# Second message pass of a two-layer GNN and FFN kernel: rows copied by VectorE into fixed buffers, ring slots freed by the last item that uses them

## The reference

```python
# src, dst: 50000 edges, sorted by dst; N = 3125 nodes, 256 features
def _L1_gnn_ref(x, W, b, edge_index):
    src, tgt = edge_index
    xt = jnp.einsum('ni,oi->no', x, W) + b
    out = jax.ops.segment_sum(xt[src], tgt, num_segments=N)
    deg = jax.ops.segment_sum(jnp.ones_like(tgt), tgt, num_segments=N)
    return out / (deg + 1.0)[:, None]

x = x + _L1_gnn_ref(_layernorm(x), W, b, [src, dst])
```

## Time and profile before

| | |
|---|---|
| timed runs (3) | median 2085.95 us, 2084.43 to 2091.15 |
| profiled execution, first to last instruction (span) | 2418.4 us |
| PE / DVE / ACT / POOL busy in the span | 57% / 39% / 19% / 46% |
| second message pass, first gather to last add | 1563.44 to 2189.47 us, 626.0 us |

### The profile page before, as it was taken

How to read it: one execution, slowest core, us unless ns; L and a number is a source line. 1 busy time by engine, 2 the same in 40 slices (tenths; PEclk the granted TensorE clock), 3 DMA queues, 4 the chain that set the end, 5 groups by cost and what they waited for, 6 DMA issues and landing times. The chain is left out here.

```text
span 2418.4 us, 23547 instructions
## 1 busy us (share of the span) xinstructions
PE 1368.5 (57%) x6436; PEld 1105.6 (46%) x6436; DVE 932.4 (39%) x1860; ACT 449.9 (19%) x1265; POOL 1109.8 (46%) x1085
## 2 busy tenths in 40 slices
PE   2512555555546136649999567035463434367988
PEld 1311433444434125549999566013342323245767
DVE  7512433333333387513333123713222222236853
ACT  0111333333334013213333122000000000002320
POOL 4276666666651400463322722173666665631530
PEclk7755667767668565679999778557666767678988
DMA  5463867677665701341111111731333332310002
GB/s 122 118 180 107 270 212 246 229 252 240 223 225 181 195 7 50 111 123 37 62 49 37 61 37 42 178 105 57 94 90 93 90 94 77 94 50 1 0 1 53
DMA packets 155861, 271.60 MB, mean 112 GB/s; under 512 B 23387, under 2 KB 118161, under 8 KB 154625
## 3 DMA queue, kind: packets, MB, share of 16 engines
q0 software_dynamic: 46128, 123.83, 17.2%
q1 hardware_dynamic: 91516, 127.72, 16.6%
q10 hardware_dynamic: 18103, 18.59, 3.4%
HBM read 172.86 MB, written 98.14 MB: 112 GB/s over the span
## 5 line engine op out<-in xcount | busy, mean ns | idle before, releaser
L1119 PE MATMUL bank<-sum_rows,sum_hot 128*125 x896 | 279.6, 469 | 384.5 <-issue 300.9
L1098 POOL DMA_INDIRECT sum_rows<-xn_tab,src_e x392 | 372.6, 951 | 271.0 <-issue 111.3
L739 POOL DMA_INDIRECT gat_rows<-xh_tab,src_e x364 | 349.1, 959 | 196.4 <-issue 103.6
L1119 PEld LDWEIGHTS bank<-sum_rows,sum_hot 128*125 128x125 f32 x896 | 193.9, 231 | 468.0 <-issue 437.4
L811 PE MATMUL bank<-gat_rows,gat_same 128*128 128x264 f32 x784 | 280.5, 500 | 171.8 <-issue 166.6
L811 PEld LDWEIGHTS bank<-gat_rows,gat_same 128*128 128x128 f32 x784 | 179.6, 250 | 218.4 <-issue 178.5
L1145 DVE TENSOR_TENSOR sums<-sums,bank 125x256 f32 x224 | 94.3, 421 | 452.5 <-remote 258.9
L1719 PE MATMUL bank<-weights,e_xthigh 128*128 x896 | 225.1, 334 | 59.2 <-issue 53.8
L855 ACT COPY gat_outs<-bank 128x264 f32<-128x264 f32 x392 | 145.8, 382 | 311.4 <-PE bank L811 231.2
L1719 PEld LDWEIGHTS bank<-weights,e_xthigh 128*128 128x128 f32 x896 | 157.6, 196 | 70.5 <-issue 70.5
L1841 DVE TENSOR_TENSOR e_h<-e_gated,bank 128x342 f32<-128x342 f32 x112 | 57.1, 510 | 335.1 <-ACT e_gated L1789 309.7
(11 more groups left out here) (483 smaller groups left out, 2320.9 us busy)
## 6 DMA issues: line engine op xcount, KB each, us to landing
parts<-gat_outs SPq DMA_DIRECT2D x28, 1904.0 KB
staged<-w_tab SPq DMA_DIRECT2D x8, 2132.0 KB
w_tab<-w_stage SPq DMA_DIRECT2D x16, 682.0 KB
w_raw<-in_L_ffn_w_dram SPq DMA_DIRECT2D x16, 640.0 KB
gat_rows<-xh_tab,src_e POOLq DMA_INDIRECT x392
sum_rows<-xn_tab,src_e POOLq DMA_INDIRECT x392
w_tab<-w_stage SPq DMA_DIRECT2D x8, 768.0 KB
w_raw<-in_L_ffn_w_dram SPq DMA_DIRECT2D x8, 682.0 KB
```

The costliest lines, as they stand in the source:

```text
L739: pool.indirect_dma_start(out=rows[b % R][:, t, :], out_offset=None, in_=k.xh_tab, in_offset=bass.IndirectOffsetOnAxis(ap=k.src_e[:, b * S ...
L1098: pool.indirect_dma_start(out=rows[:, at // IP % (RING * GPAIRS), at % IP, :], out_offset=None, in_=k.xn_tab, in_offset=bass.IndirectOffse ...
L1119: m = nc.tensor.matmul(k.ps[s][0:P, 0:C], hot[u][:, s, c, :], rows[:, bass.ds(slot, 1), c, :].rearrange("p a c -> p (a c)"), start=(c == 0 ...
```

## The change

DVE copies the two row blocks of each item (128 x 512 elements, fp32) from its ring slot into one of seven fixed buffers `held`; PE reads `held` and `hot` at constant addresses and has no register loads left. DVE does this in `stage(n)`, seven items ahead of the adds: first seven copies, then one behind each add. The reading of slot and batch and the wait for `landed` move from PE to DVE, in front of the copy; the batch is now read for every fourth item. The ring slot is free when the last item that uses the batch is staged: `walk_room` holds that item's number + 1 for each batch, and SP, three batches later (`AHEAD`), reads it, waits for `staged`, and raises `room`, on which POOL waits. The eight copies of `Prep` that ACT made go to DVE. `walk_room` costs one DVE instruction over 49 elements in the phase before.

```diff
+        v.tensor_scalar(self.room[:, :], self.ends[0:1, GPAIRS - 1:PAIRS:GPAIRS], 1.0, None, ALU.add)
...
-    def on_scalar(self, act):
-        s_, att = self.k.nc.scalar, self.k.att
-        for j in (0, 1, 2, 3, 4, 5, 12, 13):
-            act.wait_ge(self.made, j + 1)
...
+        if j < 2:
+            v.tensor_copy(self.wt[:, j, :], self.room[:, :]).then_inc(self.kept, 1)
+        elif j < 6:
+            v.tensor_copy(self.w_xt[:, j - 2, :], self.room[:, :]).then_inc(self.kept, 1)
+        elif j >= 12:
+            v.tensor_copy(att["bias"][:, (j - 12) * C:(j - 11) * C], self.room[0:P, :]).then_inc(self.kept, 1)
...
+        held = sb("held", [EP, IB, IP, C])
...
+        def wait_landed(eng, n):
+            last = min(n + LAND, ISLOTS) - 1
+            eng.wait_ge(landed, eng.value_load(w.batch[0:1, last:last + 1], min_val=1, max_val=GBATCHES))
...
             for b in range(GBATCHES):
+                if b >= AHEAD and b - AHEAD < GBATCHES - RING:
+                    sp.wait_ge(staged, sp.value_load(w.room[0:1, b - AHEAD:b - AHEAD + 1], min_val=1, max_val=ITEMS))
+                    sp.sem_inc(room, 1)
                 sp.wait_ge(rows_in[b % RING], 16 * GB * (b // RING + 1))
                 sp.sem_inc(landed, 1)
...
                 if b >= RING:
-                    pool.wait_ge(sums, GPAIRS * (b - RING) + GPAIRS - 1 + NT)
+                    pool.wait_ge(room, b - RING + 1)
...
-                        slot = pe.value_load(w.slot[0:1, n:n + 1], min_val=0, max_val=RING * GPAIRS - 1)
-                        if s % LAND == 0:
-                            last = n + min(LAND, IB - s) - 1
-                            pe.wait_ge(landed, pe.value_load(w.batch[0:1, last:last + 1], min_val=1, max_val=GBATCHES))
-                        pe.wait_ge(added, n + 1)
-                        for c in range(IP):
-                            m = nc.tensor.matmul(k.ps[s][0:P, 0:C], hot[u][:, s, c, :], rows[:, bass.ds(slot, 1), c, :].rearrange("p a c -> p (a c)"),
-                                                 start=(c == 0), stop=(c == IP - 1))
...
+                    pe.wait_ge(added, n + 1)
+                    pe.wait_ge(staged, n + 1)
+                    for c in range(IP):
+                        m = nc.tensor.matmul(k.ps[s][0:P, 0:C], hot[g % 2][:, s, c, :], held[:, s, c, :], start=(c == 0), stop=(c == IP - 1))
+                    m.then_inc(sums, 1)
...
+            def stage(n):
+                pair = ring_pair(dve, n)
+                if n % LAND == 0:
+                    wait_landed(dve, n)
+                dve.wait_ge(sums, n + 1)
+                v.tensor_copy(held_pair(n), pair).then_inc(staged, 1)
...
+                    dve.wait_ge(sums, n + 1 + IB)
                     dve.wait_ge(added, n + IB)
                     into = tile_of(k.sums, node)
                     v.tensor_tensor(into, into, k.ps[s][0:P, 0:C], ALU.add).then_inc(added, 1)
+                    if n + IB < ISLOTS:
+                        stage(n + IB)
```

More of the change, by code:

```diff
@@ L873 @@
 LAND = 4
+AHEAD = 3
 HD = 64
@@ L889, in __init__ @@
         self.slot, self.node, self.batch = sb("slot", [1, ISLOTS], I32), sb("node", [1, ISLOTS], I32), sb("batch", [1, ISLOTS], I32)
+        self.room = sb("room", [1, GBATCHES], I32)
         self.consts, self.lasts, self.reached, self.summed, self.found, self.spread, self.picked, self.laid = (
@@ L1046, in on_vector @@
         j = self.step_before(g)
-        if j is None or not 6 <= j < 12:
+        if j is None:
             return
@@ L1075, in sum_phase @@
         rows = sb("rows", [EP, RING * GPAIRS, IP, C])
+        held = sb("held", [EP, IB, IP, C])
         hot = [sb(f"hot{s}", [EP, IB, IP, P]) for s in range(2)]
         rows_in = [k.gather_sem(f"sum_rows_in{s}") for s in range(RING)]
-        landed, hot_made, sums, added, lanes = (sem(n) for n in ("landed", "hot_made", "sums", "added", "lanes"))
+        landed, staged, room, hot_made, sums, added, lanes = (
+            sem(n) for n in ("landed", "staged", "room", "hot_made", "sums", "added", "lanes"))
         lane = k.ps[IB][:, 0:P]
@@ L1082, in sum_phase, with ring_pair, held_pair @@
         block = ctx.enter_context(nc.Block())
+        def wait_landed(eng, n):
+            last = min(n + LAND, ISLOTS) - 1
+            eng.wait_ge(landed, eng.value_load(w.batch[0:1, last:last + 1], min_val=1, max_val=GBATCHES))
+        def ring_pair(eng, n):
+            slot = eng.value_load(w.slot[0:1, n:n + 1], min_val=0, max_val=RING * GPAIRS - 1)
+            return rows[:, bass.ds(slot, 1), :, :].rearrange("p a i c -> p (a i c)")
+        def held_pair(n):
+            return held[:, n % IB, :, :].rearrange("p i c -> p (i c)")
         @block.sync
@@ L1102, in _ @@
         def _(pe):
[L1103 to L1112, removed]
-                        slot = pe.value_load(w.slot[0:1, n:n + 1], min_val=0, max_val=RING * GPAIRS - 1)
-                        if s % LAND == 0:
-                            last = n + min(LAND, IB - s) - 1
-                            pe.wait_ge(landed, pe.value_load(w.batch[0:1, last:last + 1], min_val=1, max_val=GBATCHES))
-                        pe.wait_ge(added, n + 1)
-                        for c in range(IP):
-                            m = nc.tensor.matmul(k.ps[s][0:P, 0:C], hot[u][:, s, c, :], rows[:, bass.ds(slot, 1), c, :].rearrange("p a c -> p (a c)"),
-                                                 start=(c == 0), stop=(c == IP - 1))
-                        m.then_inc(sums, 1)
-        @block.scalar
-        def _(act):
-            prep.on_scalar(act)
+            pe.sem_inc(sums, IB)
+            for g in range(ITURNS):
+                pe.wait_ge(hot_made, g + 1)
+                j = prep.step_before(g)
+                if j is not None:
+                    pe.wait_ge(added, g * IB + 1)
+                    prep.on_tensor(pe, j)
+                for s in range(IB):
+                    n = g * IB + s
+                    pe.wait_ge(added, n + 1)
[3 more added lines that the diff above has]
+                    m.then_inc(sums, 1)
         @block.vector
@@ L1130, in _, with mark, add @@
             dve.sem_inc(added, IB)
[L1132 to L1134 removed]
+            def mark(g):
+                v.tensor_tensor(hot[g % 2][:, :, :, :], lane.rearrange("p (a b n) -> p a b n", a=1, b=1).to_broadcast([EP, IB, IP, P]),
+                                w.local[:, g * IB:(g + 1) * IB, :].rearrange("p i (c n) -> p i c n", n=1).to_broadcast([EP, IB, IP, P]),
                                 ALU.is_equal).then_inc(hot_made, 1)
[L1137 removed]
+            def stage(n):
[4 more added lines that the diff above has]
+                v.tensor_copy(held_pair(n), pair).then_inc(staged, 1)
+            def add(g):
                 prep.on_vector(dve, g)
@@ L1145, in add @@
                     v.tensor_tensor(into, into, k.ps[s][0:P, 0:C], ALU.add).then_inc(added, 1)
+                    if n + IB < ISLOTS:
+                        stage(n + IB)
             v.tensor_copy(lane, k.lane[:, 0:P]).then_inc(lanes, 1)
             dve.wait_ge(lanes, 1)
-            mark(0, 0)
-            for i in range(ITURNS // 2 - 1):
-                mark(i * 2 + 1, 1)
-                add(i * 2, 0)
-                mark(i * 2 + 2, 0)
-                add(i * 2 + 1, 1)
-            mark(ITURNS - 1, 1)
-            add(ITURNS - 2, 0)
-            add(ITURNS - 1, 1)
+            mark(0)
+            for n in range(IB):
+                stage(n)
+            for g in range(ITURNS):
+                if g + 1 < ITURNS:
+                    mark(g + 1)
+                add(g)
 def gather_rows(pool, into, table, row, rows_in, tiles):
```

15 lines of the change are left out of this document (2 added, 13 removed).

## The result

| | median (range), us | runs |
|---|---|---|
| before | 2084.43 (2081.66 to 2091.15) | 5 |
| changed | 2096.75 (2091.64 to 2103.73) | 5 |

The ratio is 1.0076, with a 95% interval of 1.0056 to 1.0096: slower by 0.76%. That is 12 us by the medians and 16 us by the ratio; +24 was forecast, and 2098 to 2135 us for the case that the forecast took for its own.

A forecast was written before the change was run, and what follows sets the result against it. POOL's gathers bound the phase: gathers 490 + 8, landing 2 and drain 23 make 523 us against 504, plus 5 for two engines waiting on each other. That is +24 us, 2085.95 + 24 = 2110 us; range 2000 to 2170.

The forecast's parts named there:

- the case that the forecast took for its own: Whole kernel: spells only in profiles, gathers bound, change slower at 2098 to 2135 us; chance 0.37.
- the ring of two engines: POOL and DVE waiting for each other in the ring lose 5 us where their stalls don't coincide.
- PE's register work is hidden behind the gathers: In timed runs PE needs 1.10 us per item, gathers deliver one in 2.23, so removing register work gains nothing.
- The port: DVE's copies beside POOL's gathers: 8 us more for POOL; rival at full price +107 us, 2193 us, chance 0.07.
- The drain: Behind the last landing: 8 copies, two batch reads, 15 adds and a `mark` on DVE, 23 us against 12.
- the landing: From the end of the eighth gather to PE's start, at the start of the phase: 2 us.
- The steps of `Prep`: 14 steps passing through DVE, 1.6 us each with PE's item behind, 22 us of DVE time.
- PE's spells: Stretches where PE takes 7.0 us per item instead of 1.10; taken for a cost of profiling, absent from timed runs.
- The prediction's test for itself: Signs: profiled phase 626 to 525 to 535 us, POOL's waits 99 to under 30, yet no gain in timed runs.
- Nothing to be seen: Rival: a quarter of the spells real, or chain hidden and port free; within 6 us of 2086; chance 0.14.
- the spells are in the timed runs: Rival: PE's slow stretches are real, phase 626 to 530 us, -96 us, 1990 us; chance 0.29.
- VectorE as the bound: Rival: gathers closer than 1.25 us in timed runs, DVE's 474 us decide; +40 to +98 us; chance 0.13.

The follow-up runs named there:

- idle_copies: Kernel before plus one unneeded 128 x 512 SBUF copy on DVE behind each add: 2432.78 us, ratio 1.0040 to before.
- fixed_all: Changed kernel with tile, slot, batch and room taken from the item's number, so DVE and SP load no register: 2085.66 us, ratio 1.0001 to before.
- fixed_tile: Changed kernel with each item's tile fixed at build time, one load chain less on DVE: 2097.01 us, ratio 1.0050 to before.
- copy_act_c: Changed kernel with row copies, their loads and landing waits moved from DVE to ACT, in the condition 2085: 2081.81 us, ratio 0.9992 to before.
- before_again: Kernel before, unchanged, profiled a second time, in the condition 2420: 2401.72 us (1 run), beside 2420.64 for before.
- before_c: Kernel before, unchanged, profiled a third time, in the condition 2085: 2083.17 us (1 run), beside 2084.00 for before.
- half_after: Changed kernel without every second gather from the ninth batch on (228 gathers): 2357.65 us (1 run), beside 2419.04 for before.
- copy_act: Changed kernel with row copies, their loads and landing waits moved from DVE to ACT, in the condition 2420: 2433.33 us, ratio 1.0061 to before.
- steps_act: Changed kernel with the eight copies of `Prep` left on ACT, in the condition 2420: 2496.37 us, ratio 1.0317 to before.

## Why the prediction was right, and where it was wrong

**The sign and the mechanism.** The forecast was a phase of 504 us before and 528 after (523, and 5 for the ring of two engines); it measured 506.0 and 520.3. The forecast said that PE's register work is hidden behind the gathers, and PE lost 448 address operations and all its loads without the phase getting shorter by anything. It said that freeing slots exactly is worth nothing: POOL waits for no room in either kernel.

**The port**: 8 us forecast, 5.7 measured, with bounds of 0 and 96. The mean gather is 959 to 965 ns in the seven runs that copy on DVE and have all the gathers, and 947 to 951 in the six that don't, the one ahead of the prediction included. idle_copies isolates it, in the condition 2420; in the other no timed run does, and fixed_all, with gathers of 959 ns, is level with before within its interval of 3 us. The Trainium skill's rule ("SBUF — State Buffer", section "SBUF: two separate sides": an fp32 copy locks GpSimd out of the shared ports until VectorE is done) has the direction right. If every copy held up a gather for its whole length it would have cost 96 us (the prediction's estimate, 224 x 0.427), and no run here is near that; the longest gather is 1214 ns against 1190 without the copies. What decides is the moment, by the counts under idle_copies: most gathers are held up that have a copy running as they begin, or beginning 0.4 to 0.5 us into them, and none to speak of by a copy that begins in their first 0.4 us. It looks as if a gather needed what it shares with DVE for short times only; that is read off the times and not tested.

**The drain**: 23 us forecast against 12 before, 21.0 against 12.2 measured, with the 8 copies and 15 adds of the forecast. An item costs DVE 1.58 us where 0.83 + 0.80 was put down. fixed_tile and fixed_all take the drain back to about 12 us by taking chains off DVE, copy_act_c by taking chains and copies. The port gives 5.7 and the drain 8.8 of the 14.3 us of the profiles; the landing is 0.2 shorter. In timed runs the drain by itself shows less clearly (fixed_tile).

**The ring of two engines**: 5 us forecast, nothing measured. This is the mis-sized term that matters most. With it, the port 2.3 us too dear and the drain 2.2, and 0.2 for the landing, the forecast of +24 comes down to the 14.3 of the profiles. DVE does have its slack, 53.6 us of waits for landings, and POOL never met a full ring. The steps of `Prep` were put down at 1.6 us of DVE each. What PE would wait in them was not put down: it stood up to 15.7 us in such a step, and POOL waited for none of it.

**The step that was wrong** is the inference on which, in the prediction's words, the whole forecast hangs: that PE's spells are "a cost of being profiled". The two reasons given there (332.5 us to be accounted for, and no unit in the rows that slows a 46 ns operation) spoke for a cause that no row showed. They are a condition of the session. They are there without a profiler (before_again), and they are absent from a profiled run in the other condition (before_c). (The 6.2 us of the Trainium skill, "Runtime: NRT & Kernel Launch", the preamble/postamble breakdown, that the prediction held against 332.5 are of the profile's total, not of the span from first to last instruction. In every run on record the span is 1.7 to 1.8 us below the time of the same run, and that is what 2418.4 us should have been held against.) The prediction's test for itself misled too: it said the profiled phase would shrink from 626 to 525 to 535 us, POOL's waits from 99 us to under 30, and the span to about 2320 us. The first two are 520.3 us and 0. The span is 2095.0 us, 225 below, and that was the sign that the second profile lacked more than the spells of this phase. The kernel before shrinks the same way when it is profiled in that condition (506.0, 0), and the changed one in the other doesn't (699.2 us, 127.9). The two figures came out near because the second profile was taken in another condition. The time came out in the range because the timed runs were of the condition that the reasoning about "a timed run" had assumed, and that part is luck: in the condition 2420 the change costs 75 us and not 24. Slower it is in both.

**The rivals.** "Nothing to be seen", within 6 us of before, did not come about (12 to 16 us). That the spells are in the timed runs was right in one of the two conditions, and its price was wrong even there: with the spells, the change is 3.2% slower and not 96 us faster, since register work that leaves PE lands on DVE and is slow there. Neither the prediction nor this rival asked what the slow instructions would do to the engine that receives them. VectorE as the bound was not seen in the condition 2085: gathers are 1.25 us apart, 1.27 with copies beside them, and POOL never stands. Whether DVE alone would need 474 us for the phase could not be measured, as half_after ran among spells.

**What stays open.** What the condition 2420 is. Of the 319 us between the spans of before_again and before_c, 107 are in this phase and 215 ahead of it; the stretch behind it is 3 us shorter. The gathers of the first message pass take 580 to 595 us there and 502 to 504 in the other. No instruction of a register chain reaches 0.6 us outside this phase, not even among the 896 of PE at L1719 (before_again), so slow register operations are only one part of it. Two obvious causes find no support in the traces. The packets that load the engines' code are as many in both (64 and 50, 0.2% and 0.1% on the pages of before_again and before_c), and those of the phase take about as long each (medians 1.1 and 0.4 us, against 1.0 and 0.3). The mean granted TensorE clock of the runs is 0.72 to 0.74 against 0.77 to 0.79, but queues of DVE and ACT are slow too, while DVE's adds keep their 0.42 us. Why gathers on POOL would slow another engine's queue, only in some sessions, no run shows. Nor is it shown what picks the queue: copy_act has as many register operations as the changed kernel and twice as many that last 0.6 us or more. fixed_tile and fixed_all were to tell, and both ran in the condition that has no spells. steps_act was not timed in the condition 2085, so what the eight steps cost there is known only from POOL never waiting.

## What to carry to other kernels

Work taken from an engine that the bound already hides is worth nothing, and the engine that receives it can bring two prices of its own: what it does to the bound's transfers, and what it adds behind the last of them. Where a copy must be made beside GpSimd's gathers, try the engine that neither slows them nor sits at the end of the chain, here ScalarE, even if its copy is slower. And before any wait in a profile is used, its span is to be compared with the timed runs: if they are far apart, the two are not of the same machine state, and one more profile is worth more than any argument about the difference.

## What the runs showed of the hardware that was not expected

- The same program takes 2085 or 2420 us on one and the same chip; two thirds of the difference lie ahead of this phase, one third in it, none behind it. In the condition 2420 instructions of a queue that last 23 or 46 ns last 0.7 or 1.4 us in spells while gathers stream; DVE's adds (0.42 us) and the gathers (947 ns, 1.25 us apart) don't change. Of the register operations that start more than 3 us after the last gather ended, 0.7% are slow; of the others, 13%.
- Such spells move with the register chains: 188 slow operations on PE and 11 on DVE before (before_again), 165 on DVE and none on PE after, 203 on ACT and 129 on DVE with the copies on ACT.
- The gap between the profile's span and the time of the same run is 1.75 us (2095.0 and 2096.75; 2081.4 and 2083.17), where the Trainium skill ("Runtime: NRT & Kernel Launch", the preamble/postamble breakdown) puts about 6.2 between the profile's total, which is not this span, and the reported time.
- An fp32 copy of 128 x 512 from SBUF to SBUF lasts 427 ns on DVE and 617 on ACT, and only the first lengthens gathers beside it, by 5.7 us over 392. In the eight profiles with such copies on DVE, 284 of 476 gathers with a copy running as they begin are over 955 ns, and 1 of 405 whose copy begins in their first 0.4 us.
